# A three-part attention kernel: two units share an output bank, and both ScalarE copies move between two exponentials

## The reference

```
Q1, Q2 = (Q[..., :Dh], Q[..., Dh:])        # Dh = 8, 16 heads: 32 score maps a sequence
A1 = where(causal, Q1 K1^T / sqrt(Dh), -inf);  A2 = the same with Q2, K2
attn = softmax(A1) - lam * softmax(A2)
O = attn @ V                               # 16 columns a head
O = O / sqrt(mean(O * O) + EPS) * rms_scale * (1 - LAMBDA_INIT)
X = X + O @ Wo
```

## Time and profile before

| | us |
|---|---|
| median of 3 runs | 430.4 |
| lowest, highest | 430.38, 431.64 |
| span of the profiled execution | 432.2 |
| PE busy in it | 370.7 (86%) |
| DVE busy | 308.1 (71%) |
| ACT busy | 241.8 (56%) |
| POOL busy | 198.9 (46%) |

### The profile page before, as it was taken

One profiled execution on the slowest core, in us unless ns is written; L12 is line 12 of the kernel. 1 busy time (PEld: TensorE's weight loads), 2 busy tenths in 40 slices (PEclk: granted clock), 3 DMA queues, 4 the chain that ended last, 5 costly groups with the idle time before them and its releaser, 6 DMA issues.

```text
span 432.2 us, 10129 instructions
## 1 busy us (share of the span) xinstructions
PE 370.7 (86%) x3380; PEld 240.4 (56%) x3380; DVE 308.1 (71%) x994; ACT 241.8 (56%) x585; POOL 198.9 (46%) x319
## 2 busy tenths in 40 slices
PE   0699794697999878898998788999989989999996
PEld 0566494585555544554554454555856655664774
DVE  5586852258799788797979789785665789998210
ACT  3343341034688778686877678783755243353822
POOL 6223421002468576475858567580026557883000
PEclk9999999589799999999999999999999999999999
DMA  7879999940455434244554500000000000000011
GB/s 213 260 249 333 271 237 284 216 82 2 73 78 79 77 52 69 35 79 74 76 77 77 77 5 3 3 4 0 2 0 2 1 0 2 0 1 2 18 32 49
DMA packets 47347, 34.50 MB, mean 80 GB/s; under 512 B 20033, under 2 KB 41665, under 8 KB 47297
## 3 DMA queue, kind: packets, MB, share of 16 engines
q1 hardware_dynamic: 47296, 33.86, 36.7%
HBM read 25.20 MB, written 8.39 MB: 78 GB/s over the span
## 4 chain that ended last, share of the span: by engine, by line
PE 48%; DVE 19%; issue 10%; SPq 8%; ACT 6%; DMA 4%; POOL 4%; DVEq 0%; POOLq 0%
PE ps L1370 6%; PE ps L1161 5%; PE ps L1361 5%; PE ps L1085 4%; DVE arena L1503 3%; SPq L408 3%; PE ps L1093 3%; ACT arena L827 3%; PE ps L1080 3%; DVE arena L1022 2%; DVE arena L1516 2%; PE ps L376 2%; DMA stacks<-arena 2%; PE ps L1207 2%; PE ps L645 2%
## 5 line engine op out<-in xcount | busy, mean ns | idle before, releaser
L779 POOL TENSOR_SCALAR_AFFINE_SELECT arena<-arena 128x256 f32<-128x256 f32 (+1 forms) x192 | 90.6, 485 | 94.2 <-ACT arena L827 90.3
L827 ACT ACTIVATE arena<-ps 128x512 f32<-128x512 f32 x192 | 109.2, 604 | 27.6 <-PE ps L1119 26.8
L1022 DVE TENSOR_REDUCE arena<-ps 128x4 f32<-128x1024 f32 x64 | 78.2, 1222 | 12.3 <-PE ps L1093 10.2
L1015 DVE CUSTOM_DVE_ANT_0 ps<-ps,future 128x128 f32<-128x128 f32 x256 | 66.4, 321 | 19.2 <-PE ps L1080 19.0
L1444 POOL TENSOR_TENSOR arena<-arena 128x1024 f32<-128x1024 f32 x16 | 34.1, 2132 | 40.3 <-DVE arena L1529 40.3
L1119 PE MATMUL ps<-stacks 50*128 50x256 bf16 x256 | 50.5, 278 | 0.9 <-ACT arena L827 0.8
L1085 PE MATMUL ps<-stacks 48*128 48x256 bf16 x256 | 40.6, 276 | 2.0 <-DVE arena L1022 1.5
L1161 PE MATMUL ps<-arena,values 128*17 128x256 f32 x512 | 41.0, 392 | 0.1
L473 POOL TENSOR_TENSOR qk_parts_sb<-qk_rest,qk_parts_sb 128x512 bf16<-128x512 f32 x16 | 19.0, 1208 | 40.2 <-DVE qk_parts_sb L558 40.2
L1015 DVE DVE_READ_ACCUMULATOR2_ANT arena<- 128x1 f32 x256 | 36.3, 142 | 0.1
L1574 PE MATMUL ps<-arena,upto 128*128 128x384 f32 x96 | 36.0, 487 | 0.0
(11 more groups left out here) (140 smaller groups left out, 726.0 us busy)
## 6 DMA issues: line engine op xcount, KB each, us to landing
stacks<-qk_parts SPq DMA_DIRECT2D x96, 128.0 KB, 4.7
qk_parts<-qk_parts_sb SPq DMA_DIRECT2D x16, 384.0 KB, 5.2
arena<-in_L_ffn_fc_B_dram SPq DMA_DIRECT2D x4, 1024.0 KB, 7.6
arena<-in_L_ffn_fc_A_dram SPq DMA_DIRECT2D x16, 256.0 KB, 4.9
xs<-in_L_attn_a_X_dram SPq DMA_DIRECT2D x4, 256.0 KB, 4.0
qk_parts<-qk_parts_sb SPq DMA_DIRECT2D x8, 128.0 KB, 6.1
stacks<-arena SPq DMA_DIRECT2D x64, 4.0 KB
out_dram<-xs SPq DMA_DIRECT2D x4, 256.0 KB, 2.3
```

Of the source, the lines that this page charges most:

```text
L779: nc.gpsimd.affine_select(out=diag, in_=diag, compare_op=ALU.is_ge, fill=0.0, base=0, pattern=[[0, 2 if s < 2 else UMAPS], [1, P]], channe ...
L827: nc.scalar.activation(probs[:, r, s, :], ps[:, bank, :], ACT.Exp, scale=SCALE).then_inc(exp_done, 1)
L1015: last = nc.vector.tensor_tensor_reduce(out=block, in0=block, in1=future[:], scale=1.0, scalar=LOWEST, op0=ALU.add, op1=ALU.max, accum_out ...
L1022: nc.vector.tensor_reduce(out=rowmax[:, gs, 1, UMAPS * uu:UMAPS * (uu + 1)], in_=ps[:, S_BANK + 1:S_BANK + 3, :].rearrange("p b (m k) -> p ...
```

## The change

Two consecutive units (a pair) now share one output bank: the even unit writes columns 0 to 255, the odd one columns 256 to 511. ACT copies a pair at once (128x512), PE transposes it with four transposes in a row into the whole M bank, and ACT copies 128x272 of them out. So there are 32 copies of each kind where there were 64, with as many transposes as before. A pair's products are copied in even slots, and its transposes and second copy stand in odd slots. The places move too:

- on ACT both copies now stand between the first and the second exponential of a slot, together with the copy of the normalised transposes (`columns`);
- on PE the four transposes stand behind `both(0)`, ahead of `weigh_values`; they no longer stand at the slot's end;
- the transposes of the normalised output move from the end of slot 6 to slot 2 of the next eight, behind `weigh_values`, and the output projection from slot 7 to slot 3; the other steps of a sequence come one slot later (reciprocal in slot 1, mean in 4, root in 5, normalise in 6). The last two sequences have lags of their own, and the tail has 16 slots (as before);
- `m_bank_read` makes each writer of the M bank wait for all its last readers.

```
-L_SHIFT, L_EXP, L_PV, L_OT = 4, 6, 8, 9
-L_DEN, L_DIFF, L_SQ, L_MS, L_ROOT, L_NORM, L_OPT, L_OPROJ, L_STAT = 16, 17, 19, 19, 20, 21, 22, 23, 23
+L_SHIFT, L_EXP, L_PV, L_COPY, L_OT = 4, 6, 8, 9, 10
+L_DEN, L_DIFF, L_SQ, L_MS, L_ROOT, L_NORM, L_OPT, L_OPROJ, L_STAT = (
+    (17, 17, 16), (18, 18, 17), (20, 20, 19), (20, 20, 19), (21, 21, 20), (22, 22, 21),
+    (26, 23, 22), (27, 24, 23), (27, 24, 23))
...
+        def copied_pair(it, j):
+
+            n = unit(it, j, L_COPY)
+            if in_tail(it) and j > 0:
+                n = unit(it, j, L_PV)
+            return n // 2 if n % 2 == 1 and 0 <= n < UNITS else None
+
+        def transposed_pair(it, j):
+
+            n = unit(it, j, L_OT)
+            return n // 2 if n % 2 == 1 and 0 <= n < UNITS - 2 else None
...
+            def between(it, j):
+
+                if not in_tail(it):
+                    copy_products(it, j)
+                    copy_outputs(it, j)
+                    columns(it, j)
+                squares(it, j)
+                inverse_root(it, j)
...
             def emit(it, j):
                 both(it, j, 0)
+                output_transposes(transposed_pair(it, j))
                 if live(unit(it, j, L_PV), UNITS):
                     for t in range(TPS):
                         weigh_values(it, j, t)
+                row_maxima(it, j)
+                normed_transposes(it, j)
+                output_projection(it, j)
+                both(it, j, 1)
+                both(it, j, 2)
+                score_masks(it, j)
+                output_transposes(last_pair(it, j))
...
+            def m_bank_read():
+
+                if used["shift_lo"]:
+                    pe.wait_ge(shift_lo, used["shift_lo"])
+                if used["o_copied"]:
+                    pe.wait_ge(o_copied, used["o_copied"])
+                if used["oT_done"]:
+                    pe.wait_ge(oT_done, used["oT_done"])
+                if used["resid_done"]:
+                    pe.wait_ge(resid_done, FIRST + used["resid_done"])
+
+            def output_transposes(p):
+                if p is not None:
+                    m_bank_read()
+                    pe.wait_ge(ot_copied, p + 1)
+                    for t in range(TPS):
+                        for u in range(2):
+                            at = u * SEQ + t * P
+                            last = nc.tensor.transpose(ps[:, M_BANK, (2 * t + u) * P:(2 * t + u + 1) * P],
+                                                       ot_sb[:, p % 2, at:at + P], ident[:])
+                    last.then_inc(ott_done, 1)
+                    used["o_copied"] = p + 1
```

More of the change, by code:

```diff
@@ L704, in turns @@
                         head(j)
-            for j in range(L_STAT - UPS + 1):
+            for j in range(TAIL_SLOTS):
                 amid(j)
@@ L718, in group, with due, last_pair @@
             return (SLOTS // UPG) * it + (j - lag) // UPG
-        def seq(it, j, lag):
-            return (SLOTS // UPS) * it + (j - lag) // UPS
+        def due(it, j, lags):
+            body, next_to_last, last = lags
+            for b in range(SEQS):
+                lag = last if b == SEQS - 1 else next_to_last if b == SEQS - 2 else body
+                if SLOTS * it + j == UPS * b + lag:
+                    return b
+            return None
+        def copied_pair(it, j):
[6 more added lines that the diff above has]
+            return n // 2 if n % 2 == 1 and 0 <= n < UNITS - 2 else None
+        def last_pair(it, j):
+            return PAIRS - 1 if SLOTS * it + j == LAST_OT else None
         def shifts_before(it, j):
@@ L836, in emit @@
                 if not live(n, UNITS):
[L837 to L851, removed]
+                    between(it, j)
+            def between(it, j):
[5 more added lines that the diff above has]
+                inverse_root(it, j)
@@ new lines, in copy_products, with copy_outputs @@
+            def copy_products(it, j):
+                p = copied_pair(it, j)
+                if p is not None:
+                    act.wait_ge(pv_done, 2 * p + 2)
+                    if past(p - 1):
+                        act.wait_ge(ott_done, p - 1)
+                    nc.scalar.copy(ot_sb[:, p % 2, :], ps[:, O_BANK + p % 2, :]).then_inc(ot_copied, 1)
+            def copy_outputs(it, j):
+                p = transposed_pair(it, j)
+                if p is not None:
+                    b, i = p // PPS, p % PPS
+                    act.wait_ge(ott_done, p + 1)
+                    if i == 0 and past(b - 1):
@@ L920, in residual @@
             def residual(it, j):
-                b = seq(it, j, L_OPROJ)
-                if (j - L_OPROJ) % UPS == 0 and live(b, SEQS):
+                b = due(it, j, L_OPROJ)
+                if b is not None:
                     dve.wait_ge(oproj_done, b + 1)
@@ L928, in mean_squares @@
             def mean_squares(it, j):
-                b = seq(it, j, L_MS)
-                if (j - L_MS) % UPS == 0 and live(b, SEQS):
+                b = due(it, j, L_MS)
+                if b is not None:
                     dve.wait_ge(sq_done, b + 1)
@@ L985, in tail_squares @@
             def tail_squares(it, j):
-                b = seq(it, j, L_SQ)
-                if (j - L_SQ) % UPS == 0 and live(b, SEQS):
+                b = due(it, j, L_SQ)
+                if b is not None:
                     dve.wait_ge(post, FIRST + 4 * b + 4)
```

176 lines of the change are left out of this document (77 added, 99 removed).

## The result

| | changed kernel |
|---|---|
| median of 4 runs | 437.2 us (436.53 to 438.43) |
| ratio to before, 95% interval | 1.0146 [1.0105, 1.0186] |
| span of the profiled execution | 435.7 us |
| forecast | 434.8 us, range 426.5 to 439.5 |

The change makes the kernel 1.5% slower. (Single executions of every kernel here come out 1 to 2% above the others; the ratios leave them out, the medians in us do not.) A run's time is its span plus about 1.7 us (435.7 and 437.42 here), so the profiled execution of before, with a span of 432.2, stood some 3.5 us above the median of its kernel. Where that lies shows in a second profile of the same kernel, taken later: span 428.7, time 430.39. Its reduction of slot 10 starts at 113.03, not at 116.09. What follows takes the same time in both, within 0.5 us.

The account below looks back on a forecast made before the run. DVE was taken to bound an ordinary slot at 2.33 us, with a PE and ACT loop of 2.26 close behind. The profiled 432.2 plus 2.9 and 1.6 gave 436.7, less 1.8 to the median: 434.8 us forecast, range 426.5 to 439.5.

Parts of the forecast that it names:

- rival A: The predicted outcome: slower as worked out, 432 to 438 us, chance 0.45.
- The second loop: A slot's path through PE and ACT, first score to next first score, put at 2.26 us against DVE's 2.33.
- (c): Odd slots: four transposes between first scores and `weigh_values` add 0.56 us, making an ordinary odd slot 2.82 instead of 2.33.
- rivals B and C: B: insertion costs 0.44, 430.6 us, no change, chance 0.20. C: DVE still bounds odd slots, 423 us, chance 0.20.
- (a): Slot 6: normalised transposes find the M bank free, removing a 2.06 us stall in six slots, 12.4 us at most.
- (d): Shift slots 0 and 4: shift half and 512-wide copy delay the second exponential, to 2.31 us where ready at 1.87.
- (b): ACT: merged copies save 0.17 us a pair, priced at nothing; 4.6 us for first copies if idle cover were gone.
- ACT's busy time falls by some 9 us: Predicted sign in the profile: ACT is busy some 9 us less, without any gain in time.
- The body, +2.9: Slots 11 to 63, reduction to reduction: 160.6 us forecast where before takes 157.7.
- 2.0 of them stay: Body: of 3.3 us of waits for the shift's DMA in three slots, 2.0 were forecast to remain.
- The tail, +1.6: After the body: a moved sequence's 1.65 plus 1.68 for three odd slots, less 1.2 of stalls and some 0.5.

## Why the prediction was right, and where it was off

The direction and its mechanism held (rival A). The difference forecast was +4.5 (2.9 and 1.6); by the ratio it is 1.46% of 430.4, +6.3, with an interval of 4.5 to 8.0, so the forecast difference lies at its lower edge. The time was inside the range, 2.4 above the forecast. That the sum was made against a slow profile does no harm, since it took over only a difference, but the sentence on the median should have said that a run's time is 1.7 above its span.

- **The second loop is nearly as long as DVE's.** Right. The piece from exponential to first score was taken as 0.72 and is 0.73; the wait stands in 53 slots.
- **(c) The insertion, 0.56.** Right: 0.59 (179.78 to 180.37), and an odd slot without other work is 2.86 where 2.82 was forecast. Doubled, it costs its full price in every odd slot, so rivals B and C fall. The price of 0.44 was seen here only for four more transposes behind the first four.
- **(a) The stall.** Right: 4.81 became 2.86 in slot 7, and the new slot of the projection is 4.14. Slots 2 and 3 were forecast at 6.87 together and are 7.01.
- **(d) The held exponential.** Right: slots 0 and 1 are 5.91 against 5.85, slots 4 and 5 are 6.43 against 6.35, and with the copy elsewhere the two odd ones fall by 0.40 and 0.26. Its undoing gave 2.9 of body back, less than these, since slot 6 then rose by 0.33 and slot 58 once by 1.1.
- **(b) ACT's time at nothing.** Nearly right: 1.0 us of body at most, not 4.6. The Trainium skill's figure (Perfetto Trace Analysis, Optimizing Scalar/DVE Operations) gave an estimated 2.8 us of ACT time for the 54 copies, and this trace agrees with it: splitting them again adds 2.7 to ACT's busy time, and two halves hold ACT 0.05 longer than one whole. But hardly any of that reaches the time. Its sentence that breaking up instructions may help where they cause bubbles on other engines isn't borne out here: split at the same places, the body is 1.0 longer. The waits come from where the copy and its transposes stand.
- **ACT's busy time falls by some 9 us.** Wrong: 241.8 before, 241.3 after. Split again the copies make it 244.0, so the merging takes off 2.7, and the new places add 2.2. I had taken 0.17 a pair from listed durations (two of 0.38 against one of 0.59). But successive copies overlap: each half is listed with 0.34 to 0.36, and their starts are 0.26 apart. Start to start the saving is 0.05, so durations must not be summed.
- **The body, +2.9.** It was 2.3 to 2.7, but two errors cancel in it. The period is 24.5 instead of 24.34, five times 0.2. And "2.0 of them stay", of the DMA waits, is wrong: 0.2 stay. I counted only a delay of the steps ahead of the transfer. In slot 26 the transfer is issued sooner, 2.54 after the reduction of slot 23 (154.22) and not 3.60 (154.95 before), since the moments have left the place ahead of DVE's part of the shift. In slot 54 it is issued later, 3.60 and not 3.12 after the reduction of slot 51, but the odd slot between the shift and the score that wants its data is longer too (2.93 where it was 2.79), and the issuing took 2.7 in place of 3.4. These waits come and go between the kernels (0.9 in each of two with the transposes in the hole), so they belong to no step alone.
- **The tail, +1.6.** This is the term that was mis-sized: +2.6. It was made of 1.65 for the sequence moved there and 1.68 for three insertions, less 1.2 for stalls that go and 0.5 for work done while PE would have waited. Without pairs the moved sequence alone takes the tail from 158.5 to 160.7: 2.2, not 1.65. Pairs add 0.4 to that (161.0), where the sum had them at nothing. That doesn't clear the insertion, since doubled it adds 2.1 to the tail; moved to the slot's end it doesn't shorten the tail (161.35) because it then waits for DVE's copy. These two make the 1.0. The credit was too large as well: of the stalls of the earlier trace rows the 0.44 is gone, but that of 0.56 is there again, as 0.71. In the tail of the changed kernel, in PE's timeline:

```profile
285.07 1.16 PE L1278 MATMUL ps<-wo,arena 128*128 128x128 f32 x8
...
291.72 1.98 PE L1403 MATMUL ps<-a1T,w 128*128 128x512 f32 x4
...
302.35 0.63 PE L1242 MATMUL ps<-ident,arena 128*128 128x128 f32 x4 [0.71 <-DVE xs L960]
```

The last pair's transposes wait 0.71 for DVE's residual, the last reader of the bank that the projection ahead of them fills. The first feed-forward product starts 17.05 after the reduction of slot 63 (274.67), where before it started 14.64 after (288.40 less 273.76). Ahead of it the sixth sequence's projection (285.07) now stands, which before ran within the body. That is 2.4 later; at the group of eight such products that follows (308.10, before 305.07) the lag is 2.1, and 0.4 more come in the second attention, where one wait of PE for ACT is 1.71 (353.21) and was 1.29. In the kernel without pairs that wait is 1.30. Why pairs lengthen it stays open.

- **What the prediction left out.** Sharing the banks doubles what DVE clears in them once, in slot 7 of the first eight. The changed kernel:

```profile
103.43 0.91 DVE L1090 MEMSET ps<- 128x1024 f32 x1 [0.21 <-issue]
```

and the kernel before, in its second profile:

```profile
102.85 0.48 DVE L1054 MEMSET ps<- 128x512 f32 x1
```

The gap of that slot is 3.16 instead of 2.62: 0.54 in the head, which I took to be untouched. Body 2.5, tail 2.6 and this make 5.6; the rest, up to 6.3, is inside the interval.

Left open: what shared banks are worth if every step stands in a place that costs nothing. The three kernels with the transposes in the hole keep about 4.1 in slot 3. Their bodies are 5 to 6 us shorter than that of before, but their tails are 2.8 to 3.1 longer and the clearing costs 0.5, and so they come out at the time of before or next to it. Why the clock stays low longer in one execution than in another isn't shown.

## What to carry to other kernels

Find the loops that close a step and compare their lengths: where two are within 0.1 us of each other, as DVE's 2.33 and the 2.26 of PE and ACT were, an instruction costs its full price or nothing according to whether it stands in the hole where its engine waits anyway, and how many there are hardly counts. When a change cures a rare conflict and rearranges the common step, do the cure alone first: here, in places of its own, it gave 1.6%, and the whole rearrangement cost 1.5%. Count what a step moved out of the last round of a pipeline costs in the tail: here 2.2 us for 2.0 saved. And take the price of merged instructions from starts, not from listed durations.

## What the runs showed of the hardware

Behind waits of PE of 9.01 and 7.71 us its granted clock was 0.50 to 0.54; eight 128x128 products of f32 took 1.92 at 0.54 and 1.06 at 1.00. Transposes in a row have a first price and a running one: four 128x128 transposes of f32 between narrow and value products take 0.59 from their start to the next instruction's, eight take 1.03. DVE's clearing of PSUM goes by width, 0.48 for 512 columns and 0.91 for 1024. ACT's copy of 256 columns from PSUM holds it for 0.26, of 512 columns for 0.47, when another follows, though the rows list 0.34 to 0.36 and 0.56.
